# Four half tiles of the gated layer placed in the last attention round, the last output tiles on two banks, the lookup decode one chunk later

## The chip, the cores and the metric

The kernel runs on one core of a Trainium2 chip. The metric is the time of one execution on the device in microseconds, and the median of several executions is compared. The profile shows one further execution. Engines are named as in the profile: PE is TensorE (the matrix engine), DVE is VectorE, ACT is ScalarE, POOL is GpSimd, and SP issues most of the DMA transfers.

## The reference

Eight sequences of 256 tokens (2048 tokens in all, width 512) run through a tower of five stages, each with a residual sum and, from the second on, a layer norm of its input. What matters here are the last two:

```python
# stage 4: block attention, 16 heads of 128
q, k, v = hidden @ Wq, hidden @ Wk, hidden @ Wv      # per head
p = softmax(mask(q @ k.T * D ** -0.5))               # 256 tokens: the gate keeps every earlier block
h = h + (p @ v).reshape(B, S, H * D) @ Wo
# stage 5: gated feed-forward whose weights are looked up in a table of 16 floats
x = layernorm(h)
gate = x @ lut[gate_idx].T                           # 512 -> 1376
up   = x @ lut[up_idx].T                             # 512 -> 1376
h = h + (silu(gate) * up) @ lut[down_idx].T          # 1376 -> 512
```

Every product of the last two stages is made of f16 halves: both operands are split into a high and a low half, and three matmuls (high by high, high by low, low by high) stand for one in full precision.

## The kernel before, in words

**Tiles and chunks.** `h` holds all 2048 tokens as 16 tiles of 128. A chunk is 512 tokens, so there are four. The layer norm of a tile is a short chain over four engines: DVE takes statistics (L503 or L1247), aggregates (L509) and adds the epsilon (L511); POOL takes the power -0.5 (L516); DVE writes the normed rows (`ln_dve_x`, L525); PE transposes them in four matmuls (`ln_pe`, L536); ACT writes the high half (`ln_act`, L544) and DVE the low half (`ln_dve_lo`, L551) of `tokT`, which is what the next projections read.

**Block attention.** `mo_rounds` (L1142) is a loop in hardware over two pairs of head groups (`Fori` over p = 0, 1). One pair is 8 steps (s) of 4 rounds (j), written out. A round on PE (`mo_pe`, L1152) holds: the next round's query projection (L239, 12 matmuls), one value projection (L1101, 12), the next key projection (12) with the transposes of this round's probabilities inside it (L261, 6), probabilities by values (`mo_pv`, L1135 and L1138, 12 small ones), one output tile of the step before (`mo_out`, L1114, 12) and the next round's scores (L251 and L253, 12). DVE and ACT do softmax and the splits beside it. In the last two steps of the last pair each round also transposes a layer norm tile of the next stage (chunks 0 and 1), under an `If` that the first pair skips. In the last step of the last pair there are no value projections, and in its last round (s = 7, j = 3) no next round at all: PE waits for the probabilities, transposes them, waits for their split, does `mo_pv`, the output tile and one layer norm transpose.

**Between the stages.** Behind the rounds come, on PE, the four layer norm transposes of chunk 2 and the last four output tiles (`mo_out_tail`, L1119, line of its matmuls L1127), in banks 7, 6, 2 and 3 of PSUM. DVE adds each to `h` (`mo_dve_acc`, L1219), then takes the layer norm of chunk 3.

**Gated layer.** The 1376 hidden units are 11 tiles in three groups of 4, 4 and 3. A step t is one group for one chunk, 12 steps in all. `gl_pe_proj(t)` (L1271, matmuls L1289) makes for each hidden tile m a gate half and an up half, 12 matmuls each, in banks 0 and 1 for even tiles and 2 and 3 for odd ones; ACT takes the silu (L1313), DVE the product (L1327), ACT the high half (L1317), DVE the low half (L1329). `gl_pe_out(t)` (L1296, matmuls L571 in `out_tile`) makes four output tiles in banks 6, 7, 6, 7; the third waits until DVE has added the first to `h` (`accumulate`, L576), the fourth waits for the second. PE's order is proj(0), proj(1), out(0), proj(2), out(1) and so on. DVE's is the same idea one step shifted: the tiles of step t, then the four additions of step t-1. Chunk 3's layer norm transposes stand behind the hidden tiles of step 1.

**Lookup decode.** Weights of groups 0 and 1 were decoded long before; POOL splits them to halves (`gl_w`, L899 and L903; group 0 inside the second pair of attention, group 1 after the last layer norm). The 18 blocks of group 2 are decoded by DVE during the gated layer. `gdec_step(t, at)` (L2005) is called behind each hidden tile (at = 0 to 3) and each addition (at = 4 to 7) of step t, and writes out by hand which block b is masked (L859 to L864), spread (L873) and picked (L881) there; POOL splits each block (L890, L892) and counts `gfree`. PE waits for all 18 (`gfree`) ahead of proj(8). The indices come by one DMA (L1838), which SP issues once all attention outputs are there. SP's later transfers are one weight load (L1840) and the stores of the result (L1844, L1847).

The `If` that runs in the last pair only is this helper; ahead of the transposes a wait on the layer norm count stands under it:

```python
def last_pair(eng, p, pairs):
    return eng.If(p > pairs - 2)
```

## Time and profile before

| | |
|---|---|
| median of 3 executions | 2463.64 us (2461.04 to 2465.51) |
| profiled execution, its own time | 2462.3 us |
| its span | 2460.3 us |
| PE busy | 2323.6 us, 94% |
| DVE, ACT, POOL busy | 67%, 32%, 15% |
| chain that ended last | PE 80%, DVE 12%, ACT 4% |

Times in rows are microseconds from the start of the span. A row of a timeline gives the start, the length, engine, line, operation, tiles and shapes, the count of instructions merged in it, and in brackets the idle time ahead of it with what ended it. PE's instructions are pipelined: the next group starts a little before the modelled end of the one in front, so the pace is read from start to start.

### The profile page before, as it was taken

To read this page: it belongs to the slowest core of one execution; us is meant where nothing else is said; L and a number is where in the kernel's file an instruction comes from. 1 tells how busy PE (TensorE), PEld (TensorE's weight loads), DVE (VectorE), ACT (ScalarE), POOL (GpSimd) and SP (SyncE) were. 2 spreads that over 40 slices of the span, in tenths; PEclk is the share of its full clock that TensorE was granted. 3 is DMA by queue.
4 is the path that set the end of the run, shared out by engine and by line. 5 is a ranking of instruction groups with operands and counts; after the bars stand their busy time and mean duration, and the time that the engine had idled before them with its cause. 6 is when DMAs were issued, how large, how long until landed. Compare 5 with 4: busy or idle time off the path is not lost.

```text
span 2460.3 us, 32611 instructions
## 1 busy us (share of the span) xinstructions
PE 2323.6 (94%) x12610; PEld 1202.9 (49%) x12610; DVE 1654.4 (67%) x3165; ACT 788.6 (32%) x1683; POOL 376.2 (15%) x416
## 2 busy tenths in 40 slices
PE   5877799999999999889999999999999997999999
PEld 3666444444444444434455555555555554444444
DVE  6577599998999787676465555555555565778623
ACT  5576412122121113333343333333333332211111
POOL 2353100000000412630040004002100300411000
PEclk9898899999999999999999999999999998999999
DMA  4554623333332440200020001001100100100001
GB/s 161 171 172 171 227 92 114 125 121 114 122 120 86 163 165 33 78 31 19 27 69 1 1 1 69 1 2 35 35 1 1 52 1 1 56 1 1 1 1 69
DMA packets 50799, 166.71 MB, mean 68 GB/s; under 512 B 4048, under 2 KB 16976, under 8 KB 41680
## 3 DMA queue, kind: packets, MB, share of 16 engines
q1 hardware_dynamic: 50640, 164.56, 18.9%
q8 instruction: 103, 1.69, 0.3%
q14 instruction: 56, 0.46, 0.1%
HBM read 137.28 MB, written 27.26 MB: 67 GB/s over the span
## 4 chain that ended last, share of the span: by engine, by line
PE 80%; DVE 12%; ACT 4%; issue 2%; POOL 1%; DMA 1%; SPq 0%; DVEq 0%; ACTq 0%
PE ps L678 19%; PE ps L239 13%; PE ps L1289 7%; PE ps L690 7%; PE ps L1114 6%; PE ps L1101 6%; PE ps L571 4%; PE ps L929 3%; PE ps L946 3%; PE ps L1135 2%; PE ps L253 2%; PE ps L408 2%; PE ps L261 2%; PE ps L251 1%; PE ps L536 1%
## 5 line engine op out<-in xcount | busy, mean ns | idle before, releaser
L678 PE MATMUL ps<-planes 128*128 128x512 f16 x1224 | 270.0, 379 | 1.4 <-DVE work L735 1.4
L678 PE MATMUL ps<-planes,wa 128*128 128x512 f16 x1080 | 239.2, 380 | 5.2 <-DMA wa<-rw 5.2
L239 PE MATMUL ps<-planes,wa 128*128 128x512 f16 x840 | 201.5, 385 | 5.1 <-DVE planes L1576 5.1
L678 PEld LDWEIGHTS ps<-planes 128*128 128x128 f16 x1224 | 119.5, 98 | 143.4 <-DVE work L735 2.3
L239 PE MATMUL ps<-planes 128*128 128x512 f16 x768 | 180.9, 379 | 1.5 <-issue 1.5
L718 ACT ACTIVATE work<-work 128x512 f16<-128x512 f32 x64 | 40.3, 630 | 442.2 <-DVE work L751 442.2
L678 PEld LDWEIGHTS ps<-planes,wa 128*128 128x128 f16 x1080 | 106.0, 98 | 131.6 <-issue 7.5
L516 POOL TENSOR_TENSOR rstd<-rstd,half 128x4 f32<-128x4 f32 x16 | 17.1, 1071 | 871.1 <-DVE rstd L511 871.1
L294 ACT ACTIVATE ps<-ps,nmax 128x128 f32<-128x128 f32 x160 | 54.5, 341 | 295.4 <-DVE nmax L288 295.3
L833 DVE COPY_PREDICATED work<-work 128x1024 f32<-128x1024 int16 x144 | 120.4, 836 | 21.6 <-DVE work L833 0.8
L946 PE MATMUL ps<-wa,work 128*128 128x512 f16 x512 | 124.6, 387 | 9.0 <-DVE h L976 9.0
L815 DVE TENSOR_SCALAR work<-work,lutx,par 128x256 int32<-128x256 int32 x384 | 132.7, 421 | 0.0
L929 PE MATMUL ps<-planes,wa 128*128 128x512 f16 x512 | 126.0, 391 | 4.0 <-POOL wa L1059 4.0
L239 PEld LDWEIGHTS ps<-planes,wa 128*128 128x128 f16 x840 | 83.2, 99 | 93.2 <-issue 5.7
L1289 PE MATMUL ps<-planes 128*128 128x512 f16 x528 | 116.9, 379 | 2.6 <-DVE work L1327 2.6
L1289 PE MATMUL ps<-planes,wa 128*128 128x512 f16 x528 | 116.6, 379 | 0.0
L239 PEld LDWEIGHTS ps<-planes 128*128 128x128 f16 x768 | 75.1, 98 | 78.7 <-issue 1.7
L318 DVE TENSOR_TENSOR work<-ps,work 128x768 f16<-128x768 f32 x76 | 72.7, 956 | 47.4 <-ACT work L314 47.4
L1219 DVE TENSOR_TENSOR h<-ps,h 128x512 f32<-128x512 f32 x64 | 44.3, 692 | 83.5 <-PE ps L1114 76.9
L966 DVE TENSOR_TENSOR work<-work 128x512 f16<-128x512 f32 x64 | 49.1, 778 | 74.4 <-ACT work L962 74.4
L899 POOL TENSOR_SCALAR planes<-stg 128x512 f16<-128x512 f32 x44 | 30.9, 728 | 437.8 <-PE ps L1114 416.5
L301 DVE RECIPROCAL rinv<-rsum 128x4 f32<-128x4 f32 x80 | 14.2, 177 | 120.0 <-ACT ps L296 120.0
(193 smaller groups left out, 4442.3 us busy)
## 6 DMA issues: line engine op xcount, KB each, us to landing
planes<-rw SPq DMA_DIRECT2D x17, 2048.0 KB, 7.9
wa<-rw SPq DMA_DIRECT2D x15, 2048.0 KB, 7.3
stg<-in_rw_w SPq DMA_DIRECT2D x32, 512.0 KB, 3.8
stg<-in_ff_w SPq DMA_DIRECT2D x16, 1024.0 KB, 5.1
rw<-wa SPq DMA_DIRECT2D x16, 1024.0 KB, 7.0
stg<-in_mo_w SPq DMA_DIRECT2D x16, 1024.0 KB, 4.8
work<-in_glu_idx SPq DMA_DIRECT2D x48, 128.0 KB, 2.1
glu_dec<-work SPq DMA_DIRECT2D x48, 128.0 KB, 1.7
```

The costliest lines, as they stand in the source:

```text
L239: mm = te.matmul(ps[:, bank, :], w(i, kt), x(j, kt), start=(kt == 0 and n == 0), stop=(kt == KT - 1 and n == 2))
L318: ve.tensor_tensor(pT[1].rearrange("p (b k) -> p b k", b=2), pT_view, pT[0].rearrange("p (b k) -> p b k", b=2), ALU.subtract).then_inc(pT_ ...
L571: mm = te.matmul(ps[:, bank, :], x, y, start=(m == 0), stop=(m == len(pairs) - 1))
L678: mm = te.matmul(ps[:, what, :], rw_w(q, what, i, kt, m), mix[what][j][:, kt, at:at + CH], start=(kt == 0 and z == 0), stop=(kt == KT - 1 ...
L690: mm = te.matmul(ps[:, 4 + j, :], oT[t % 4][x][:, j * P:j * P + P], rw_wo(q, y, m), start=(n == 0 and z == 0), stop=(n == HEADS - 1 and z ...
L815: return ve.tensor_scalar(dec_v[:, j, :].bitcast(I32), dec_idx, lutx[:, j:j + 1], lut[:, 2 * j:2 * j + 1], ALU.bitwise_and, ALU.bitwise_xor)
L833: ins = ve.copy_predicated(pairs[:, :, 0, :], mask, pairs[:, :, 1, :])
L929: mm = te.matmul(ps[:, t % 3, :], slot[:, at:at + P], tokT[x][:, kt, c * CH:c * CH + CH], start=(kt == 0 and x == 0), stop=(kt == KT - 1 a ...
L946: mm = te.matmul(ps[:, 4 + j, :], gT[t % FF_BUF][x][:, j * P:j * P + P], slot[:, PW + m * D:PW + m * D + D], start=(k == 0 and x == 0), st ...
L1101: mm = te.matmul(ps[:, bank, :], tokT[x][:, kt, tt * P:tt * P + P], halves(slot, 2)[y][:, kt * CH:kt * CH + CH], start=(kt == 0 and z == 0 ...
L1114: mm = te.matmul(ps[:, FB, :], x, y, start=(z == 0), stop=(z == len(pairs) - 1))
L1289: mm = te.matmul(ps[:, bank, :], glu_halves(g, piece)[i][:, at:at + P], tokT[j][:, kt, c * CH:c * CH + CH], start=(kt == 0 and z == 0), st ...
```

## The change

It has three parts. Four half tiles of proj(0) (gate and up of hidden tiles 0 and 1) leave `gl_pe_proj` and are placed one by one: both halves of tile 0 ahead of the probability transposes of the last round, the gate half of tile 1 between these and `mo_pv`, the up half of tile 1 behind the rounds; their silus, products and splits are placed between the layer norm pieces of chunk 2. The last four output tiles use banks 7, 6, 7, 6, so the third and fourth wait for the additions of the first and second, each tile is placed one place earlier relative to the transposes, and the wait for all four additions, which stood ahead of hidden tile 1, stands ahead of out(0). `gdec_step` starts one step later: block 0 at the additions of step 1, and blocks 16 and 17 at the hidden tiles of step 7.

```diff
@@ -1114,7 +1114,7 @@
                 mm = te.matmul(ps[:, FB, :], x, y, start=(z == 0), stop=(z == len(pairs) - 1))
             mm.then_inc(mw_ps, 1)
 
-        TAIL_BANK = [FB, OB, 2, 3]
+        TAIL_BANK = [FB, OB, FB, OB]
 
         def mo_out_tail(pe, tt, slot):
 
@@ -1122,6 +1122,8 @@
             if tt == 0:
                 pe.wait_ge(mo_lo, n)
                 pe.wait_ge(mw_acc, n + 4)
+            if tt >= 2:
+                pe.wait_ge(mw_acc, n + 4 + tt - 1)
             pairs = [(oH[1][j][x][:, tt * P:tt * P + P], halves(slot, 3)[y][:, j * D:j * D + D]) for j in range(4) for x, y in PASSES]
             for z, (x, y) in enumerate(pairs):
                 mm = te.matmul(ps[:, TAIL_BANK[tt], :], x, y, start=(z == 0), stop=(z == len(pairs) - 1))
@@ -1166,7 +1168,12 @@
             if rcond is None:
                 mo_q(pe, *nround, 1, transposes)
             else:
+                with last_pair(pe, p, MO_PAIRS):
+                    gl_pe_part(pe, 0, 0, 0)
+                    gl_pe_part(pe, 0, 0, 1)
                 transposes()
+                with last_pair(pe, p, MO_PAIRS):
+                    gl_pe_part(pe, 0, 1, 0)
                 with Maybe(pe, rcond):
                     mo_q(pe, *nround, 1)
             mo_pv(pe, p, s, j)
@@ -1268,34 +1275,36 @@
         def gl_rows(g, m):
             return G_LAST if g == 2 and m == 2 else P
 
+        def gl_pe_part(pe, t, m, piece):
+            g, c = GL_T[t]
+            n = gl_base(t) + m
+            if m == 0 and piece == 0 and c == 0:
+                if g < 2:
+                    pe.wait_ge(w_ready, WR_GL + 3 * g + 3)
+                else:
+                    pe.wait_ge(gfree, GDEC_BLOCKS)
+            if n >= 2 and piece == 0:
+                pe.wait_ge(prod_sb, n - 1)
+            for kt in range(KT):
+                for z, (i, j) in enumerate(PASSES):
+                    at = kt * G_TILES[g] * P + m * P
+                    mm = te.matmul(ps[:, 2 * (n % 2) + piece, :], glu_halves(g, piece)[i][:, at:at + P],
+                                   tokT[j][:, kt, c * CH:c * CH + CH], start=(kt == 0 and z == 0),
+                                   stop=(kt == KT - 1 and z == 2))
+            mm.then_inc((ga_ps, up_ps)[piece], 1)
+
         def gl_pe_proj(pe, t):
-            g, c = GL_T[t]
-            if c == 0 and g < 2:
-                pe.wait_ge(w_ready, WR_GL + 3 * g + 3)
-            elif c == 0:
-                pe.wait_ge(gfree, GDEC_BLOCKS)
-            for m in range(G_TILES[g]):
-                n = gl_base(t) + m
-                if n >= 2:
-                    pe.wait_ge(prod_sb, n - 1)
-                elif n == 1:
-                    pe.wait_ge(mw_acc, 8 + 64)
-                W = G_TILES[g] * P
-                for piece, done in ((0, ga_ps), (1, up_ps)):
-                    bank = 2 * (n % 2) + piece
-                    for kt in range(KT):
-                        for z, (i, j) in enumerate(PASSES):
-                            at = kt * W + m * P
-                            mm = te.matmul(ps[:, bank, :], glu_halves(g, piece)[i][:, at:at + P],
-                                           tokT[j][:, kt, c * CH:c * CH + CH], start=(kt == 0 and z == 0),
-                                           stop=(kt == KT - 1 and z == 2))
-                    mm.then_inc(done, 1)
+            for m in range(2 if t == 0 else 0, G_TILES[GL_T[t][0]]):
+                gl_pe_part(pe, t, m, 0)
+                gl_pe_part(pe, t, m, 1)
                 if t == 1:
                     ln_pe(pe, 3, 3, m)
 
         def gl_pe_out(pe, t):
             g, c = GL_T[t]
             pe.wait_ge(gl_lo, gl_base(t + 1))
+            if t == 0:
+                pe.wait_ge(mw_acc, 8 + 64)
             for j in range(TPC):
                 pairs = []
                 for m in range(G_TILES[g]):
@@ -1303,30 +1312,42 @@
                     pairs += [(hT[t % 2][m][x][0:r, j * P:j * P + P], glu_halves(g, 2)[y][0:r, m * D:m * D + D]) for x, y in PASSES]
                 out_tile(pe, O_GL + 4 * t + j, 6 + j % 2, pairs)
 
+        def gl_act_silu(act, t, m):
+            n = gl_base(t) + m
+            act.wait_ge(ga_ps, n + 1)
+            if n >= 2:
+                act.wait_ge(gl_lo, n - 1)
+            se.activation(sg_buf[n % 2], ps[:, 2 * (n % 2), :], ACT.Silu).then_inc(silu_sb, 1)
+
+        def gl_act_hi(act, t, m):
+            n = gl_base(t) + m
+            act.wait_ge(prod_sb, n + 1)
+            if m == 0 and t >= 2:
+                act.wait_ge(wo_ps, O_GL + 4 * t)
+            se.activation(hT[t % 2][m][0], sg_buf[n % 2], ACT.Copy).then_inc(gl_hi, 1)
+
         def gl_act(act, t):
-            g, c = GL_T[t]
-            for m in range(G_TILES[g]):
-                n = gl_base(t) + m
-                act.wait_ge(ga_ps, n + 1)
-                if n >= 2:
-                    act.wait_ge(gl_lo, n - 1)
-                se.activation(sg_buf[n % 2], ps[:, 2 * (n % 2), :], ACT.Silu).then_inc(silu_sb, 1)
-                act.wait_ge(prod_sb, n + 1)
-                if m == 0 and t >= 2:
-                    act.wait_ge(wo_ps, O_GL + 4 * t)
-                se.activation(hT[t % 2][m][0], sg_buf[n % 2], ACT.Copy).then_inc(gl_hi, 1)
+            for m in range(2 if t == 0 else 0, G_TILES[GL_T[t][0]]):
+                gl_act_silu(act, t, m)
+                gl_act_hi(act, t, m)
                 if t == 1:
                     ln_act(act, 3, 3, m)
 
+        def gl_dve_prod(dve, t, m):
+            n = gl_base(t) + m
+            dve.wait_ge(silu_sb, n + 1)
+            dve.wait_ge(up_ps, n + 1)
+            ve.tensor_tensor(sg_buf[n % 2], sg_buf[n % 2], ps[:, 2 * (n % 2) + 1, :], ALU.mult).then_inc(prod_sb, 1)
+
+        def gl_dve_lo(dve, t, m):
+            n = gl_base(t) + m
+            dve.wait_ge(gl_hi, n + 1)
+            ve.tensor_tensor(hT[t % 2][m][1], sg_buf[n % 2], hT[t % 2][m][0], ALU.subtract).then_inc(gl_lo, 1)
+
         def gl_dve(dve, t, between):
-            g, c = GL_T[t]
-            for m in range(G_TILES[g]):
-                n = gl_base(t) + m
-                dve.wait_ge(silu_sb, n + 1)
-                dve.wait_ge(up_ps, n + 1)
-                ve.tensor_tensor(sg_buf[n % 2], sg_buf[n % 2], ps[:, 2 * (n % 2) + 1, :], ALU.mult).then_inc(prod_sb, 1)
-                dve.wait_ge(gl_hi, n + 1)
-                ve.tensor_tensor(hT[t % 2][m][1], sg_buf[n % 2], hT[t % 2][m][0], ALU.subtract).then_inc(gl_lo, 1)
+            for m in range(2 if t == 0 else 0, G_TILES[GL_T[t][0]]):
+                gl_dve_prod(dve, t, m)
+                gl_dve_lo(dve, t, m)
                 if t == 1:
                     ln_dve_lo(dve, 3, 3, m)
                 between(t, m)
@@ -1932,7 +1953,13 @@
             ln_chunk(act, ln_act, 2, NC - 1)
             act_exp(act, MU)
             mo_rounds(act, lambda *x: mo_act(act, *x))
-            ln_chunk(act, ln_act, 3, 2)
+            gl_act_silu(act, 0, 0)
+            gl_act_silu(act, 0, 1)
+            ln_act(act, 3, 2, 0), ln_act(act, 3, 2, 1)
+            gl_act_hi(act, 0, 0)
+            ln_act(act, 3, 2, 2)
+            gl_act_hi(act, 0, 1)
+            ln_act(act, 3, 2, 3)
             for t in range(len(GL_T)):
                 gl_act(act, t)
 
@@ -1992,20 +2019,24 @@
 
             mo_rounds(dve, lambda *x: mo_dve(dve, *x, chain))
             ln_chunk(dve, ln_dve_x, 3, 2)
+            mo_dve_acc(dve, MO_PAIRS, 0, 0, TAIL_BANK[0])
+            gl_dve_prod(dve, 0, 0)
             ln_dve_lo(dve, 3, 2, 0), ln_dve_lo(dve, 3, 2, 1)
-            mo_dve_acc(dve, MO_PAIRS, 0, 0, TAIL_BANK[0])
+            mo_dve_acc(dve, MO_PAIRS, 0, 1, TAIL_BANK[1])
+            gl_dve_prod(dve, 0, 1)
+            gl_dve_lo(dve, 0, 0)
             ln_dve_lo(dve, 3, 2, 2)
-            mo_dve_acc(dve, MO_PAIRS, 0, 1, TAIL_BANK[1])
+            mo_dve_acc(dve, MO_PAIRS, 0, 2, TAIL_BANK[2])
+            gl_dve_lo(dve, 0, 1)
             ln_dve_lo(dve, 3, 2, 3)
-            mo_dve_acc(dve, MO_PAIRS, 0, 2, TAIL_BANK[2])
             mo_dve_acc(dve, MO_PAIRS, 0, 3, TAIL_BANK[3])
             dve.wait_ge(mw_acc, 8 + 64)
             ln_dve_chunk(dve, 3, 3, chain)
             ln_chunk(dve, ln_dve_x, 3, 3)
             def gdec_step(t, at):
 
-                b = 3 * t - 2 + (at // 2 if at < 4 else 2) if t > 0 else 0
-                if b < GDEC_BLOCKS and (t > 0 or at >= 4):
+                b = 3 * t - 5 + (at // 2 if at < 4 else 2)
+                if 0 <= b < GDEC_BLOCKS:
                     if at in (0, 2, 4):
                         gdec_dve_mask(dve, b)
                     if at in (0, 2, 5):
@@ -2041,12 +2072,13 @@
                     pe.wait_ge(mv_lo, j + 1)
                 ln_pe(pe, 2, NC - 1, j)
             mo_rounds(pe, lambda *x: mo_pe(pe, *x))
+            gl_pe_part(pe, 0, 1, 1)
+            mo_out_tail(pe, 0, weight_slot("moba", 1))
             ln_pe(pe, 3, 2, 0), ln_pe(pe, 3, 2, 1)
-            mo_out_tail(pe, 0, weight_slot("moba", 1))
+            mo_out_tail(pe, 1, weight_slot("moba", 1))
             ln_pe(pe, 3, 2, 2)
-            mo_out_tail(pe, 1, weight_slot("moba", 1))
+            mo_out_tail(pe, 2, weight_slot("moba", 1))
             ln_pe(pe, 3, 2, 3)
-            mo_out_tail(pe, 2, weight_slot("moba", 1))
             mo_out_tail(pe, 3, weight_slot("moba", 1))
             gl_pe_proj(pe, 0)
             for t in range(len(GL_T)):
```

## Rows read from the trace of the kernel before

**Rows 1.** The page: busy time and share of the engines, and TensorE's granted clock.

```profile
PE 2323.6 (94%) x12610; PEld 1202.9 (49%) x12610; DVE 1654.4 (67%) x3165; ACT 788.6 (32%) x1683; POOL 376.2 (15%) x416
...
PEclk9898899999999999999999999999999998999999
```

**Rows 2.** TensorE's timeline, last attention round: start, length, work [idle before].

```profile
2058.26 0.87 PE L261 MATMUL ps<-ident,work 128*128 128x128 f32 x6 [1.94 <-DVE work L307]
...
2061.18 0.50 PE L1135 MATMUL ps<-work,planes 128*128 128x256 f16 x3
...
2062.18 2.75 PE L1114 MATMUL ps<-wa,planes 128*128 128x512 f16 x12
...
2065.87 0.49 PE L253 MATMUL ps<-work 128*128 128x256 f16 x3
2071.53 1.52 PE L261 MATMUL ps<-ident,work 128*128 128x128 f32 x6 [5.17 <-DVE work L307]
2074.95 0.82 PE L1135 MATMUL ps<-work,planes 128*128 128x256 f16 x3 [1.90 <-DVE work L318]
```

**Rows 3.** The same, from the end of the rounds into the gated layer.

```profile
2080.22 0.60 PE L536 MATMUL ps<-ident,work 128*128 128x128 f32 x4
2085.12 1.89 PE L536 MATMUL ps<-ident,work 128*128 128x128 f32 x8 [4.30 <-DVE work L525]
2086.80 3.68 PE L1127 MATMUL ps<-wa,planes 128*128 128x512 f16 x12
2090.32 0.60 PE L536 MATMUL ps<-ident,work 128*128 128x128 f32 x4
2090.75 2.75 PE L1127 MATMUL ps<-wa,planes 128*128 128x512 f16 x12
...
2098.96 26.06 PE L1289 MATMUL ps<-planes 128*128 128x512 f16 x120
```

**Rows 4.** Two stretches of 10 us: busy by engine, then granted clock, DMA.

```profile
2070.00:2080.00 10.00, 6.57 (x29) 3.93 (x30) 4.00 (x7) 1.62 (x4) 0.00 (x0) 0.66 0.00 0
2150.00:2160.00 10.00, 4.70 (x13) 1.54 (x12) 9.20 (x22) 1.11 (x2) 1.14 (x2) 0.68 0.00 0
```

**Rows 5.** VectorE's timeline around the end of the rounds.

```profile
2070.80 0.68 DVE L307 TENSOR_TENSOR work<-ps,rinv 128x512 f32<-128x512 f32 x1
...
2084.52 1.92 DVE L525 TENSOR_SCALAR work<-h,mv,rstd 128x512 f32<-128x512 f32 x4 [1.12 <-POOL rstd L516]
...
2099.16 0.69 DVE L1219 TENSOR_TENSOR h<-ps,h 128x512 f32<-128x512 f32 x1 [1.90 <-PE ps L1127]
...
2104.10 3.09 DVE L525 TENSOR_SCALAR work<-h,mv,rstd 128x512 f32<-128x512 f32 x4 [1.12 <-POOL rstd L516]
```

**Rows 6.** TensorE's waits from 2100 us to the end: total, times, longest.

```profile
PE ps L571 <- DVE h L576: 8.1, 6, 5.3
PE ps L1289 <- DVE work L1327: 2.6, 2, 2.1
```

**Rows 7.** TensorE's timeline, outputs of chunk 0 and the projection behind them.

```profile
2155.70 7.63 PE L571 MATMUL ps<-planes,work 128*128 128x512 f16 x24 [5.30 <-DVE h L576]
2163.17 20.88 PE L1289 MATMUL ps<-planes 128*128 128x512 f16 x96
```

**Rows 8.** VectorE's timeline, one decode instruction beside GpSimd's splits and without them.

```profile
2123.80 1.19 DVE L862 TENSOR_SCALAR planes<-planes 128x256 int16<-128x256 int16 x1
...
2135.51 0.22 DVE L862 TENSOR_SCALAR planes<-planes 128x256 int16<-128x256 int16 x1
```

**Rows 9.** GpSimd's timeline: last split of group 0's weights, last lookup block.

```profile
1930.02 4.50 POOL L903 TENSOR_TENSOR planes<-stg,planes 128x512 f16<-128x512 f32 x4
...
2317.01 0.67 POOL L892 TENSOR_TENSOR stg<-planes,stg 128x256 f16<-128x256 f32 x1
```

**Rows 10.** ScalarE's timeline: its table load ahead of the first silu.

```profile
2094.60 1.28 ACT L1313 ACT_TABLE_LOAD   x1
```

**Rows 11.** TensorE's timeline where the loop over pairs goes back.

```profile
1651.94 2.75 PE L239 MATMUL ps<-planes 128*128 128x512 f16 x12 [1.47 <-issue]
```

## The prediction

> **What bounds the kernel.** I read the page first. PE is busy 94% of the span and its granted clock is 9 or 8 tenths almost everywhere [rows 1], so what can be gained lies in PE's waits, and in stretches at the low clock behind them. I then went along PE's timeline over the place that the diff touches. Up to the last round PE runs with short gaps: in the round before, transposes, probabilities by values and an output tile follow on each other at the full pace [rows 2]. In the last round there is nothing to put between them. PE waits 5.17 us for DVE's probabilities and 1.90 us for their split [rows 2], and behind the rounds 4.30 us for the layer norm rows of chunk 2 [rows 3]. The granted clock of that stretch is 0.66 [rows 4], between the levels of 1.2 and 2.4 GHz, and what follows each wait is slow: 6 transposes take 1.52 us, not 0.87 [rows 2], and an output tile 3.68 us [rows 3]. Last, PE's waits behind 2100 us come to two lines only: the output tiles wait 8.1 us in 6 places for DVE's additions, once 5.3 us, and the projections 2.6 us for its products [rows 6]. The 5.3 us end at 2155.70, and there again the clock is down (0.68 over ten microseconds, [rows 4]; 24 matmuls take 7.63 us, [rows 7]). PE alone sets the end from the last round on, so a microsecond off its waits is one off the time, as long as no other wait grows.
>
> **Part 1: the half tiles and the tail.** The pace of the gated layer is 26.06 us for 120 matmuls [rows 3], 0.217 each: 2.61 us for 12, 5.21 for 24. An output tile has the same 12 shapes, so 2.61 too. A set of 4 transposes takes 0.43 (2090.32 to 2090.75, [rows 3]), the 12 of `mo_pv` 1.00 (2061.18 to 2062.18) and the 6 transposes some 0.70 (0.87 less the 0.17 by which such a row overlaps the next, [rows 2, 3]). No matmul is added or removed. From the end of the last scores, 2066.36 (2065.87 and 0.49, [rows 2]), to the end of proj(0), 2119.8 (2098.96 and 96 x 0.217, [rows 3]), PE now takes 53.4 us. Its work at full pace is 8 half tiles 20.9, 4 tail tiles 10.4, the round's output tile 2.6, five sets of layer norm transposes 2.2, `mo_pv` 1.0, transposes 0.7: 37.8 us. If nothing waits and the clock holds, 15.6 us go: 11.4 us are the three waits, 4.2 us the low clock.
>
> Does anything wait? I lay the new order out. Two half tiles fill 2066.36 to 2071.5; the probabilities are ready when the last normalization ends, 2070.80 and 0.68 [rows 5]. So that wait is filled nearly exactly (0.1 us may stay). The half tile behind the transposes runs to some 2074.9. DVE needs the transposes' end, ACT's copy and its own split, 1.9 us of wait in all at the row's start of 2074.95; with transposes that start alike and run faster the split is there at 2074.2, so `mo_pv` starts 0.7 us later than it could, which costs nothing, since PE works. `mo_pv`, output tile and transposes then end at 2079.0 where they end now at 2080.82 (2080.22 and 0.60, [rows 3]). From that end to the first layer norm row of chunk 2 the chain over DVE and POOL takes 3.7 us to its start (2084.52, [rows 5]) and a quarter of 1.92 us more: ready at 2083.3. PE has the up half of tile 1 and the first tail tile in front, 5.2 us, to 2084.1. Slack 0.8 us: thin, and the first thing that could be late. Its price is one for one. The third and fourth tail tiles now wait for additions. DVE's order puts the first behind the four rows (2084.7), and two transposes and a tile stand between on PE until 2087.9; slack over 2 us. The layer norm transposes of tile 2 need the low half of tile 0, behind that addition and one product, near 2086.7, against 2087.6: 0.9 us. ACT has the table load, 1.28 us [rows 10], and two silus ahead of its next layer norm copy: from 2079.7 to 2082.2, and the copy is due at 2084.7. The last tail tile ends at 2093.7, not 2099.16 as now (start of the last addition, [rows 5]). Chunk 3's layer norm on DVE then takes as now to 2107.2 from 2099.16 (2104.10 and 3.09, [rows 5]), 8.0 us, so to 2101.7, and hidden tile 2's product stands behind it, near 2102.4. PE needs it at the first tile of proj(1), 2104.1. Slack 1.7 us. Weights of group 0 lie ready since 1934.5 (1930.02 and 4.50, [rows 9]), 130 us ahead. Bank 0 and 1 are free, since the last round projects no query or key. Part 1: -15.5 us.
>
> **Part 2: the decode.** In the kernel before, block 0 starts on DVE right behind the last product of step 0, while POOL is still splitting weights; one decode instruction takes 1.19 us there and 0.22 later without them [rows 8]. The block stands ahead of step 1's products, and blocks 1 and 2 between them, and the 2.6 us and the 5.3 us of waits are theirs [rows 6]. Moved a step on, step 1 has no decode until its additions. DVE's share of a hidden tile there is product, low half and layer norm half, under 3 us against PE's 5.6, so the first addition of out(0) is bound by its own tile and is done 1.8 us before PE's third tile wants it. Both waits go: 7.9 us. With them goes the low clock behind the second, 7.47 (2155.70 to 2163.17) less 5.21: 2.3 us [rows 7]. Idle figures count from a modelled end that lies 0.17 us past the pace, three times 0.5 us more. Part 2: -10.7 us. In return the decode reaches into step 7. Steps 2 to 6 now pay (8.1 - 5.3) / 5 = 0.56 us each, since the third output tile waits for an addition that stands behind a pick [rows 6]; steps 2 to 7 will, one more: +0.7 us with its 0.17. The wait for `gfree` ahead of proj(8) has its cover: the last block's split ends at 2317.68 in step 6 now [rows 9], about when PE takes up its last two output tiles, 5.2 us before the next projection. One step on it is the same. SP and its DMAs keep their order; the index load starts some 5 us earlier and is due 30 us later.
>
> **Part 3: the branches.** PE gets two new `If`s, which pair 0 skips (24 and 12 matmuls). No row has a jump of that length by itself. The nearest rows: the jump back of the loop costs 1.47 us of issue [rows 11], as upper bound each; at the `If` around 4 layer norm transposes, which pair 0 skips eight times, the same timeline shows no idle time: lower bound zero, and a gain is excluded, as instructions are only added. I take 0.3 us for both, since PE's queue is full there; 2.9 us goes into the range. The Trainium skill (Runtime: NRT & Kernel Launch, Instruction fetch mechanics) says that a taken branch beyond the window already fetched must first fetch its target. By it the sum would be the 1.47 for each jump that leaves the window: -22.6 us in place of -25.2 if both do.
>
> **The sum**: -15.5 - 10.7 + 0.7 + 0.3 = -25.2 us against the profiled execution's own 2462.3, so 2437.1. The median shown is 1.3 us above that execution: 2463.64 - 25.2 = 2438.4.
>
> **The rivals.**
> - A: a thin slack closes (layer norm rows of chunk 2, or the low half behind the first product) and each such wait gives back 1 to 3 us, with the clock down behind it as now. For it: 0.8 and 0.9 us are small against the chain of four engines. Against: all lengths are from rows. 5 us back: 2443.4.
> - B: the stalls of step 1 don't go but move, since DVE now meets step 1 with POOL's splits still running, or to out(1). For it: DVE is the releaser of every wait there. Against: ten microseconds of decode leave it. Half of part 2 back, 5.4, to all, 10.7: 2443.8 to 2449.1.
> - C: the skipped branches cost their upper bound, twice 1.47: 2441.0.
> - D: the change doesn't fill the round, because a half tile waits for something that I take as ready, and DVE's and ACT's new order only passes the waits on. Part 2 alone stays: 2463.64 - 10.7 + 0.7 = 2453.6. Against: the weights are ready 130 us ahead, and the tokens' norm is two steps back.
> - E, on the other side: the granted clock. The stretch from 2066 us on becomes nearly gapless. If PE were then granted 1.2 GHz for a long time, each such microsecond would cost half of one; beyond 50 us of it the whole gain is spent, beyond 60 us the kernel is slower than 2468.6. Against: of the 40 slices the dense ones already show 9 [rows 1], and low clock shows behind waits, not behind work [rows 4].
>
> **How the numbers follow.** My forecast has 0.62, A 0.12, B 0.10, C 0.08, D 0.04, E 0.03, and 0.01 lies elsewhere. The forecast's own range is the 2.3 us that the runs scatter on either side, and 1 us of fractions: 2435 to 2442. The 8 in 10 take in C, A and the near end of B: 2434.5 to 2446. A measurement of this kernel can tell about 0.2%, 5 us, from no change: all cases but E lie below that, D by 10 us. Faster 0.95, same 0.02, slower 0.03.
>
> **What would show it.** Right: PE without a wait over 0.3 us from the last scores to the end of out(0), the granted clock at 1.00 in ten-microsecond stretches there, proj(0) ending near 2104, proj(2) starting near 2137 in place of 2163.17 [rows 7]; six waits of 0.56 us on additions in steps 2 to 7; proj(8) without a wait. Wrong: a wait for L525 ahead of the layer norm transposes (A), one for L576 or L1327 over 1 us in step 1 (B), issue time on PE near the end of pair 0's last round (C), idle time ahead of the first half tile (D), a slice with a low clock and no idle time (E).

## The result, and the profile after

| | before | changed |
|---|---|---|
| median (range) | 2462.57 us (2461.04 to 2465.51, 4 runs) | 2438.0 us (2435.26 to 2441.05, 4 runs) |
| profiled execution | 2462.3 us | 2440.1 us (one of the four) |
| last scores of attention to start of proj(2) | 96.81 us | 70.37 us |
| start of proj(2) to PE's last matmul | 293.99 us | 294.73 us |

The ratio is 0.9896 (95% interval 0.9882 to 0.991): 24.6 us less. The prediction was 2438.4, range 2434.5 to 2446. The median before has one run more in it than the 2463.64 that the prediction started from. The last two lines of the table are read from PE's timelines: the first is from the end of the last row of L253 to the first projection behind out(0) [rows 2, 7]. They are the yardstick of everything below. The three stages ahead of attention scatter by several microseconds from one execution to the next (the first value projection of attention starts at 1218.1 us before, at 1221.7 here, and between 1215.1 and 1223.3 in the profiles of the experiments), in code that no kernel here touches; the two stretches repeat to 0.1 us in most kernels, and the exceptions have a cause, told below.

PE's timeline of the changed kernel, from the last scores to the end of out(0) and proj(2), answers to [rows 2, 3, 7]; the lines are start, length, work:

```profile
2069.37 0.49 PE L253 MATMUL ps<-work 128*128 128x256 f16 x3
2069.70 5.34 PE L1291 MATMUL ps<-planes 128*128 128x512 f16 x24
2075.03 0.88 PE L261 MATMUL ps<-ident,work 128*128 128x128 f32 x6
2075.74 2.75 PE L1291 MATMUL ps<-planes 128*128 128x512 f16 x12
...
2079.32 2.75 PE L1114 MATMUL ps<-wa,planes 128*128 128x512 f16 x12
...
2084.93 2.75 PE L1129 MATMUL ps<-wa,planes 128*128 128x512 f16 x12
2087.53 1.04 PE L536 MATMUL ps<-ident,work 128*128 128x128 f32 x8
...
2097.04 15.70 PE L1291 MATMUL ps<-planes 128*128 128x512 f16 x72
2129.87 10.52 PE L571 MATMUL ps<-planes,work 128*128 128x512 f16 x48
2140.23 20.88 PE L1291 MATMUL ps<-planes 128*128 128x512 f16 x96
...
2166.84 5.35 PE L571 MATMUL ps<-planes,work 128*128 128x512 f16 x24 [0.55 <-DVE h L576]
```


No line from 2069.37 to 2140.23 has idle time in brackets. The transposes of the probabilities take 0.88 us, the first tail tile 2.75, not 3.68 as in [rows 3]. out(0) is one row of 48 matmuls; before it was cut by 5.30 us. The wait for an addition, 0.55 us, stands in out(1) and the steps behind it.

The same place by stretches of ten microseconds (columns as in [rows 4], the granted clock third from the end):

```profile
2070.00:2080.00 10.00, 10.00 (x58) 5.20 (x57) 5.22 (x11) 3.01 (x10) 0.00 (x0) 1.00 0.00 0
2080.00:2090.00 10.00, 10.00 (x54) 5.34 (x53) 7.02 (x17) 4.80 (x8) 1.01 (x1) 1.00 0.01 2
```


And all of PE's waits over 0.2 us from 2060 us on, to set beside [rows 6] (the second line belongs to the round before the last, which no kernel here changes):

```profile
PE ps L571 <- DVE h L576: 3.4, 6, 0.6
PE ps L261 <- DVE work L307: 1.9, 1, 1.9
```


The thin places, first on DVE's timeline of the changed kernel (compare [rows 5]):

```profile
2086.21 1.92 DVE L525 TENSOR_SCALAR work<-h,mv,rstd 128x512 f32<-128x512 f32 x4 [1.12 <-POOL rstd L516]
...
2089.23 1.28 DVE L551 TENSOR_TENSOR planes<-ps,planes 128x512 f16<-128x512 f32 x2
...
2105.19 0.67 DVE L1340 TENSOR_TENSOR work<-work,ps 128x512 f32<-128x512 f32 x1
2106.55 1.39 DVE L1345 TENSOR_TENSOR work<-work 128x512 f16<-128x512 f32 x1 [0.69 <-ACT work L1327]
```

And on ACT's timeline, the table load and the first layer norm copy of chunk 2 (compare [rows 10]):

```profile
2083.16 1.28 ACT L1320 ACT_TABLE_LOAD   x1
...
2088.16 1.08 ACT L544 ACTIVATE planes<-ps 128x512 f16<-128x512 f32 x2 [2.62 <-PE ps L536]
```


The first layer norm row of chunk 2 is ready at 2086.7 (2086.21 and a quarter of 1.92), and PE takes it at 2087.53. Tile 0's low half is written at 2089.9, and PE's next transposes are due at 2090.99. Tile 0's silu waits for nothing but its table load, and the layer norm copy behind it is on time at 2088.16. Hidden tile 2's product ends at 2105.86; PE's first tile of proj(1) is due some 48 x 0.217 = 10.4 us behind 2097.04, at 2107.45.

### The profile page after: what moved, and what is told of

The parts are those of the page before. It is cut to its first block, busy times and chain, and to the rows that moved or that the text cites. A ratio compares the mean times of both kernels' runs of the same rounds, so it can differ in the third digit from the quotient of the medians.

```text
span 2438.1 us, 32615 instructions
## 1 busy us (share of the span) xinstructions
PE 2317.2 (95%) x12610; PEld 1200.4 (49%) x12610; DVE 1650.1 (68%) x3165; ACT 787.9 (32%) x1683; POOL 374.0 (15%) x416
## 4 chain that ended last, share of the span: by engine, by line
PE 81%; DVE 10%; ACT 4%; POOL 2%; issue 2%; DMA 1%; SPq 0%; DVEq 0%; ACTq 0%
PE ps L678 20%; PE ps L239 13%; PE ps L1291 8%; PE ps L690 7%; PE ps L1114 6%; PE ps L1101 6%; PE ps L571 3%; PE ps L929 3%; PE ps L946 3%; PE ps L1137 2%; PE ps L253 2%; PE ps L261 2%; PE ps L408 2%; PE ps L536 1%; PE ps L251 1%
```

## The experiments

Times are medians beside runs of the kernel before on the same chip; "the stretch" is last scores to proj(2) in the profile, "the rest" from there to PE's last matmul. Experiments 1, 4, 5, 8 and 9 start from the changed kernel, 2, 3, 6 and 7 from the one before. Kernels 4 and 6 were profiled twice; the second profiled executions took 2440.39 and 2461.9 us.

| | median, us | ratio (95%) | stretch | rest |
|---|---|---|---|---|
| before | 2461.4 to 2463.4 | 1 | 96.81 | 293.99 |
| changed, run again | 2437.04 | 0.9895 (0.9877 to 0.9913) | 70.36 | 294.67 |
| 1 half tiles and tail only | 2451.67 | 0.9958 (0.9945 to 0.9971) | 85.98 | 294.01 |
| 2 decode shift only | 2449.7 | 0.9951 (0.9938 to 0.9964) | 85.66 | 294.72 |
| 3 tail order only | 2460.1 | 0.9988 (0.9979 to 0.9996) | 92.55 | 294.00 |
| 4 hidden tile 0 only | 2443.01 | 0.9919 (0.9907 to 0.9931) | 74.39, 76.06 | 294.68 |
| 5 pick behind the addition | 2433.12 | 0.9877 (0.9859 to 0.9896) | 70.38 | 290.30 |
| 6 first wait filled | 2463.68 | 1.0006 (0.9997 to 1.0015) | 96.19, 96.37 | 293.93 |
| 7 all waits filled | 2457.95 | 0.998 (0.9971 to 0.9989) | 92.80 | 293.91 |
| 8 block 0 in step 0 | 2445.15 | 0.993 (0.9914 to 0.9946) | 79.25 | 293.95 |
| 9 the same, splits behind it | 2435.13 | 0.9886 (0.9871 to 0.9901) | 70.37 | 293.93 |

The changed kernel's second runs were expected so:

> The changed kernel itself, run beside the next three as their yardstick. Both theories: as measured, 24 to 25 us under before.

They came out so (2437.04, 24.4 us under 2461.39), with the stretch equal to 0.01 us.

### 1 and 2: each part alone

```diff
 # 1, against the changed kernel
-                b = 3 * t - 5 + (at // 2 if at < 4 else 2)
-                if 0 <= b < GDEC_BLOCKS:
+                b = 3 * t - 2 + (at // 2 if at < 4 else 2) if t > 0 else 0
+                if b < GDEC_BLOCKS and (t > 0 or at >= 4):
 # 2, against the kernel before: the same two pairs of lines, the other way round
```

> The changed kernel with the decode schedule of before (block 0 at the additions of step 0). My theory: part 1 is worth 15.5 us by itself, but block 0 now meets POOL's splits for its whole length and DVE is 0.6 us further behind PE, so the waits of step 1 stay and grow by about 1.5 us: near 2448.5 us, 14 us under before, with a wait of L1291 for DVE of 2 to 4 us and one of L571 of some 5 us. Rival (the parts simply add): 15.5 us under before, and the waits of step 1 as they were. Rival (most of the gain is the decode's): less than 8 us under before.

> The kernel of before with the decode one step later and nothing else. My theory: the 2.6 us and 5.3 us of waits in step 1 and the low clock behind them go, a sixth wait of 0.56 us comes: 10 us under before, near 2452.6 us. Rival B of the prediction (the stall moves to out(1) or the next step): 0 to 5 us under before.

Alone, the half tiles bring 10.3 us (2461.97 less 2451.67; 10.8 of the stretch) and the decode 12.3 (11.2 of the stretch, less 0.7 of the rest). The two savings add to 22.0, while both changes together take 26.4 off the stretch: 4.5 us exist only if both are made. Kernel 1 is where they went. PE's timeline of it, from the second transposes of chunk 3 on:

```profile
2113.63 0.60 PE L536 MATMUL ps<-ident,work 128*128 128x128 f32 x4
2121.40 6.85 PE L1291 MATMUL ps<-planes 128*128 128x512 f16 x24 [7.17 <-DVE work L1340]
...
2143.90 7.54 PE L571 MATMUL ps<-planes,work 128*128 128x512 f16 x24 [4.42 <-DVE h L576]
```


Its first wait of step 1 is 7.17 us, where the kernel before has 2.13 (of the 2.6 us in [rows 6]), and the low clock comes with it (a row of 24 matmuls takes 6.85 us, at full pace 5.34). I had expected 2 to 4 us. DVE's and POOL's timelines show why, first in the kernel before:

```profile
2122.00 0.70 DVE L859 CAST planes<-planes 128x256 int16<-128x256 int32 x1
...
2122.64 4.54 POOL L903 TENSOR_TENSOR wa<-stg,wa 128x512 f16<-128x512 f32 x4
...
2127.31 2.67 DVE L873 TENSOR_SCALAR planes<-planes,lutx,par 128x256 int32<-128x256 int32 x8
```

and in kernel 1:

```profile
2105.97 0.70 DVE L859 CAST planes<-planes 128x256 int16<-128x256 int32 x1
...
2115.63 6.13 POOL L903 TENSOR_TENSOR wa<-stg,wa 128x512 f16<-128x512 f32 x4
...
2115.73 5.04 DVE L881 COPY_PREDICATED planes<-planes 128x1024 f32<-128x1024 int16 x3
```

The parts don't add: PE reaches step 1 some 15 us sooner against the scores. Block 0 started 5.2 us before the splits ended in the kernel before and took 10.6 us (2122.00 to 2132.6). In kernel 1 it lies wholly beside them and takes 14.8 (2105.97 to 2120.8). The median is 3.2 us over the 2448.5 that I expected. Kernel 2 came out as expected in kind, with no wait in step 1, and a little better in size.

### 3 and 4: pieces of the first part

```diff
 # 3, against the kernel before: banks 7, 6, 7, 6, and each tail tile one place earlier
-            ln_pe(pe, 3, 2, 0), ln_pe(pe, 3, 2, 1)
             mo_out_tail(pe, 0, weight_slot("moba", 1))
+            ln_pe(pe, 3, 2, 0), ln_pe(pe, 3, 2, 1)
...
 # 4, against the changed kernel: tile 1 back in proj(0)
-                with last_pair(pe, p, MO_PAIRS):
-                    gl_pe_part(pe, 0, 1, 0)
...
-            gl_pe_part(pe, 0, 1, 1)
...
-            for m in range(2 if t == 0 else 0, G_TILES[GL_T[t][0]]):
+            for m in range(1 if t == 0 else 0, G_TILES[GL_T[t][0]]):
```

> The kernel of before with the last four output tiles each one place earlier and on banks 7, 6, 7, 6, no half tile moved, decode as before. My theory: the first tail tile (2.6 us) covers that much of the 4.3 us wait for the layer norm rows, and with it some low clock: 3 to 4.5 us under before, near 2459 us, and no wait ahead of the third and fourth tile. Rival: these two now wait for additions and give it back: within 1 us of before.

> The changed kernel with hidden tile 0 alone moved early (the two half tiles ahead of the transposes); both halves of tile 1 are back in their place. My theory: the wait ahead of the value products is open again (1.9 us less what the faster transposes save, so 1.2 to 1.9) and the wait for the layer norm rows is 4.3 less the tail tile's 2.6, so 1.7; the clock stays up: 3 to 3.6 us over the changed kernel, near 2441.3 us. Rival: the granted clock falls again behind these waits and adds 2 to 4 us: near 2444.5 us.

Kernel 3 has a stretch 4.3 us shorter, as my theory said; its median shows 1.9, with runs scattered over 8.6 us and the stages ahead of attention ending 4.9 us later in its profile than in that of before (1223.0 against 1218.1). The first tail tile does not start at once, but the wait for rows of chunk 2 is down from 4.30 to 1.11 us, plus 0.44 us until the round's last addition. The third and fourth tile wait for nothing. Kernel 4 is 4.0 us over the changed one by the stretch, 5 by the medians of different sets; the three waits open again, in PE's timeline of its first profile:

```profile
2072.94 0.50 PE L1137 MATMUL ps<-work,planes 128*128 128x256 f16 x3 [1.89 <-DVE work L318]
...
2077.57 2.75 PE L1129 MATMUL ps<-wa,planes 128*128 128x512 f16 x12 [0.44 <-DVE h L1224]
2081.43 1.11 PE L536 MATMUL ps<-ident,work 128*128 128x128 f32 x8 [1.11 <-DVE work L525]
```


1.89, 0.44 and 1.11 make 3.4, and three pipeline ends of 0.17 the rest. In this profile the clock stayed up. A second profile of the same kernel had the same three waits and a stretch of 76.06:

> The kernel with hidden tile 0 alone moved early, one more look, for the same question: fixed by the program: full pace behind the 1.9 us wait again (74.4 us from the last scores to proj(2)). Not fixed: the low clock shows there this time, and 2 to 4 us more.

PE's timeline of that second profile:

```profile
2072.47 0.50 PE L1137 MATMUL ps<-work,planes 128*128 128x256 f16 x3 [1.90 <-DVE work L318]
...
2072.98 0.73 PE L1137 MATMUL ps<-work,planes 128*128 128x256 f16 x3
...
2073.83 4.07 PE L1114 MATMUL ps<-wa,planes 128*128 128x512 f16 x12
```


The value products begin at full pace (0.50) and go on at the low one (0.73), and the output tile takes 4.07 us, not 2.75. So with short waits left in place, whether the clock falls differs between executions of one program.

### 6 and 7: the clock by itself

```diff
 # against the kernel before; 6 has the first block with filler(pe, 0), filler(pe, 1) of 12 matmuls each
+        def filler(bank, n):
+            for x in range(n):
+                te.matmul(ps[:, bank, :], glu_halves(0, 0)[0][:, x * P:x * P + P], tokT[0][:, 0, 0:CH], start=(x == 0), stop=(x == n - 1))
...
+                with last_pair(pe, p, MO_PAIRS):
+                    pe.wait_ge(w_ready, WR_GL + 3)
+                    filler(0, 12)
+                    filler(1, 12)
                 transposes()
+                with last_pair(pe, p, MO_PAIRS):
+                    filler(0, 8)
...
             mo_rounds(pe, lambda *x: mo_pe(pe, *x))
+            filler(0, 9)
+            filler(1, 9)
```

> The kernel of before with 24 matmuls more (the shapes of two half tiles, their result in banks 0 and 1 never read) in the 5.17 us wait of the last round; all real work stays where it was, the decode too. It prices the clock by itself. My theory: the low clock of that stretch was caused by the idle time, so with the wait filled the transposes, the value products and the output tile behind it run at full pace (2.4 us less), and the second wait too may end sooner: 2.4 to 4.1 us under before, though 5.2 us of work are added. Rival: the clock has nothing to do with it, or the added work only delays: 0 to 1 us over before.

> The kernel with the first wait filled, one more look. If the fall of the clock behind the 1.9 us wait is fixed by the program, the value products run at the low clock again (a row of 3 takes 0.7 us or more). If it hangs on something that differs from execution to execution, they may run at full pace (0.50), as in the kernel with tile 0 alone moved, whose PE work is the same up to there.

> The kernel of before with added matmuls of no use in all three waits (24, 8 and 18 of the 512-column shape), the decode as before. The run with the first wait alone filled gave back only 0.7 us from the last scores to the start of proj(0), since the clock fell behind the second wait instead. My theory now: the low clock belongs to the row of waits, not to one, so with all three covered the whole stretch is at full pace: 4 us less from the last scores to the start of proj(0) (28.6 us in place of 32.6), granted clock 1.00 there. Rival: the clock falls in this place whatever fills it, or the added work makes its own delay: 32 us or more.

With the first wait covered (kernel 6) the way from the last scores to proj(0) is 31.95 and 31.96 us in the two profiles, not 32.60 (2066.36 to 2098.96, [rows 2, 3]): 0.65 us saved, not the 2.4 I expected, and the median shows no gain. The transposes run at full pace, but the clock falls behind the second wait, at once in one profile and within the value products in the other. PE's timeline of the first:

```profile
2064.00 5.34 PE L1155 MATMUL ps<-planes 128*128 128x512 f16 x24
2069.34 0.87 PE L261 MATMUL ps<-ident,work 128*128 128x128 f32 x6
2072.11 0.74 PE L1135 MATMUL ps<-work,planes 128*128 128x256 f16 x3 [1.89 <-DVE work L318]
...
2073.92 3.61 PE L1114 MATMUL ps<-wa,planes 128*128 128x512 f16 x12
```


With all three covered (kernel 7) the waits that are left are 0.17 and 0.41 us, and everything up to proj(0) runs at full pace. PE's timeline:

```profile
2072.32 1.89 PE L1154 MATMUL ps<-planes 128*128 128x512 f16 x8
2074.38 0.50 PE L1135 MATMUL ps<-work,planes 128*128 128x256 f16 x3 [0.17 <-DVE work L318]
...
2078.41 4.05 PE L1154 MATMUL ps<-planes 128*128 128x512 f16 x18
2082.87 1.11 PE L536 MATMUL ps<-ident,work 128*128 128x128 f32 x8 [0.41 <-DVE work L525]
2083.82 2.75 PE L1127 MATMUL ps<-wa,planes 128*128 128x512 f16 x12
```


From the last scores to proj(0) it is 28.6 us, and the stretch is 92.80, both 4.0 us less than before (the median is 5.4 less, 2457.95 against 2463.40), with 50 useless matmuls more and not one piece of work moved. This is the clock's share of part 1, which the prediction had put at 4.2 us, now measured without the rest. Covering the first wait alone gave 0.65 us of it. Kernel 4 kept the clock in one of its two profiles with waits of 1.89, 0.44 and 1.11 us left, so filling every wait is not always needed; no kernel here covers the second or the third wait alone.

### 8 and 9: what block 0 costs

```diff
 # 8, against the changed kernel
-                b = 3 * t - 5 + (at // 2 if at < 4 else 2)
-                if 0 <= b < GDEC_BLOCKS:
+                b = 3 * t - 4 + (at // 2 if at < 4 else 2) if t > 0 else 0
+                if at >= 4 if t < 2 else b < GDEC_BLOCKS:
 # 9, besides: POOL's program
+            gdec_pool_split(pool, 0)
             gl_w(1)
-            for b in range(GDEC_BLOCKS):
+            for b in range(1, GDEC_BLOCKS):
```

> The changed kernel with only block 0 of the decode back at the additions of step 0, beside POOL's splits; block 1 at the additions of step 1, the rest three per step, block 17 alone in step 7. It tells block 0's place from that of blocks 1 and 2 among step 1's hidden tiles. My theory: the first of the two waits of step 1 comes back (2.5 to 3.5 us, with POOL beside it), the 5.3 us one does not, and one wait of 0.56 us goes: 2 to 3 us over the changed kernel. Rival: block 0 is what delays all of step 1: the 5 us wait and the low clock come back too: 7 to 10 us over the changed kernel.

> The kernel with block 0 in step 0 (8.9 us slower than the changed one from the last scores to proj(2)), and POOL's splits of group 1 moved behind block 0's own split, so that they no longer run beside block 0. Theory of contention: block 0 then takes some 6.5 us on DVE where it took 14.9 beside the splits, the 7.2 us wait of proj(1) goes to under 1 us, and the kernel is within 1.5 us of the changed one (70.4 us from the last scores to proj(2)). Rival of place: any block between the products of step 0 and step 1 delays PE: at least 4 us over the changed kernel.

Block 0 alone in step 0 costs 8.9 us of the stretch, far over my 2 to 3. The size is the rival's, but not its mechanism: out(0) is whole, and the cost is one wait of 7.19 us and 1.5 us of low clock behind it. DVE's timeline of kernel 8 shows why, with POOL's last split beside it:

```profile
2107.51 0.70 DVE L859 CAST planes<-planes 128x256 int16<-128x256 int32 x1
...
2110.16 7.08 DVE L873 TENSOR_SCALAR planes<-planes,lutx,par 128x256 int32<-128x256 int32 x8
2117.18 6.14 POOL L903 TENSOR_TENSOR wa<-stg,wa 128x512 f16<-128x512 f32 x4
2117.28 5.05 DVE L881 COPY_PREDICATED planes<-planes 128x1024 f32<-128x1024 int16 x3
2122.23 0.68 DVE L1340 TENSOR_TENSOR work<-work,ps 128x512 f32<-128x512 f32 x1
...
2141.70 2.67 DVE L873 TENSOR_SCALAR planes<-planes,lutx,par 128x256 int32<-128x256 int32 x8
```

From 2107.51 block 0 lasts until 2122.3, 14.8 us, with the eight instructions of the spread in 7.08 us and the picks in 5.05. POOL splits without a pause from 2099.09 to 2123.3. The spread of block 1, one step later and with POOL idle, takes 2.67. And DVE's timeline of kernel 9, where POOL's splits stand behind the block (the last line is their first):

```profile
2104.17 0.29 DVE L859 CAST planes<-planes 128x256 int16<-128x256 int32 x1
...
2105.23 2.67 DVE L873 TENSOR_SCALAR planes<-planes,lutx,par 128x256 int32<-128x256 int32 x8
2107.94 2.55 DVE L881 COPY_PREDICATED planes<-planes 128x1024 f32<-128x1024 int16 x3
2110.39 0.68 DVE L1340 TENSOR_TENSOR work<-work,ps 128x512 f32<-128x512 f32 x1
...
2111.70 2.80 POOL L899 TENSOR_SCALAR wa<-stg 128x512 f16<-128x512 f32 x4
```


Here the block takes 6.3 us, spread 2.67, picks 2.55. The product that PE waits for is written at 2111.1 in kernel 9, in time, and the stretch is 70.37, the same as the changed kernel's, with the block still in step 0. (Block 1 then meets the last split, its spread takes 5.42 us, but it stands between additions and nobody waits.) So block 0's cost was neither its place nor its work but the company. That is block 0 alone: kernels 1 and 8 differ only in the places of the other blocks, and the stretch by 6.7 us (85.98 against 79.25). Blocks 1 and 2 between the hidden tiles of step 1 cost that, by the 4.42 us wait of out(0) and 2.2 us of low clock behind it. Whether they would still cost it with POOL's splits out of the way was not tried.

### 5: what the changed kernel leaves

```diff
 # against the changed kernel: hidden tile 3 runs no decode; behind the additions stand
+                    if j == 0:
+                        gdec_step(t, 3)
+                    elif j == 1:
+                        gdec_step(t, 4), gdec_step(t, 5)
+                    elif j == 2:
+                        gdec_step(t, 6)
```

> The changed kernel with DVE's order turned at each step's end: the pick of the second block behind the first addition, mask and spread of the third behind the second addition. My theory: the first addition no longer stands behind a pick, so the six waits of 0.56 us of the third output tile go, each with its 0.15 of pipeline: 4.3 us under the changed kernel, near 2433.7 us. Rival: the second addition, now behind the pick, is late for the fourth tile instead: within 1 us of the changed kernel, with waits of L571 at other tiles.

4.4 us off the rest, and 3.9 us off the changed kernel's median of the same set: 2433.12, ratio to before 0.9877. DVE adds as soon as the output tile is there, and the pick fits in front of the second addition. DVE's timeline at out(2):

```profile
2196.43 0.69 DVE L576 TENSOR_TENSOR h<-ps,h 128x512 f32<-128x512 f32 x1
2197.03 2.55 DVE L881 COPY_PREDICATED planes<-planes 128x1024 f32<-128x1024 int16 x3
2199.47 0.69 DVE L576 TENSOR_TENSOR h<-ps,h 128x512 f32<-128x512 f32 x1
```


Its PE timeline has no wait over 0.2 us between the last scores and the end. This is the lowest median of the study; kernel 9, at 2435.13 beside another set, lies within the scatter of it, and the two were not put together.

## Why the prediction was right

**Part 1.** The prediction had 53.4 us from the last scores to the end of proj(0) become 37.8, and set -15.5 us. After: 2069.86 to 2107.45, 37.6 us; -15.8. The order that was laid out by hand holds piece by piece. Foreseen slacks were 0.8 us for the first layer norm row, 0.9 for tile 0's low half and 1.7 for hidden tile 2's product; they came out as 0.8, 1.1 and 1.6. The split into 11.4 us of waits and 4.2 of clock was an argument then, and kernel 7 measured the clock's share at 4.0.

**Part 2.** Set at -10.7 us; the stretch of 26.4 less part 1's 15.8 leaves 10.6. By the prediction proj(2) starts 70.6 us behind the last scores (2137 less 2066.36), and it came at 70.37. The sixth wait came as set: 6 waits of 3.4 us in all, and 0.7 us more of the rest. The wait for the last block stays covered: proj(8) starts without one. What the prediction had only half right is the cause. It named POOL's contention from one instruction (1.19 against 0.22, [rows 8]) but counted block 0 as a place in DVE's order. Kernels 8 and 9 show that block 0 in that same place costs 8.9 us beside the splits and nothing without them. In the kernel before less of it showed: only the five instructions of block 0's mask met the end of the splits and took 5.3 us (2122.00 to 2127.3), against 1.0 in kernel 9 (2104.17 to 2105.2); spread and picks ran at their full pace.

**Part 3.** The skipped branches were set at 0.3 us with 2.9 as the bound. The attention rounds up to the last scores take 848.18 us from the first value projection, 848.23 before, with two jumps more, and the jump back still costs 1.47 us of issue. In the last round of pair 0, where the two branches are skipped, PE's timeline has no idle time. The same way takes 847.4 to 848.7 us in the other profiles, 848.55 and 848.73 in kernels 2 and 3, which have no branch; so 0.3 us can't be told from nothing here, and 2.9 can. Rival C falls. The Trainium skill (Runtime: NRT & Kernel Launch, Instruction fetch mechanics) has a taken branch wait for a fetch if its target is not in the window. No run here shows where the two targets lay; by the unchanged 848.2 us no such wait reached PE's work.

**The rivals A, B, D and E** did not come. D would have shown as idle time ahead of the first half tile, and there is none at 2069.70. A was a matter of 0.8 us. B came true in kernel 1, which has the half tiles and not the decode shift: there the stall grows to 7.17 us. E falls with ten-microsecond stretches at a granted clock of 1.00 throughout.

**The sum** was -25.2 us and the measured median -24.6, the second set -24.4. The two stretches show 25.7 (26.4 less 0.7), against 25.5 set for them without the branches. That the median lies within 0.4 us of 2438.4 is luck in part: the four runs are 2435.3, 2435.9, 2440.1 and 2441.1, and the profiled one is only 22.2 us under that of before, as its attention starts 3.6 us later (1221.7 against 1218.1). My expectations for the experiments did worse than the prediction: kernel 1's wait, kernel 6's gain and kernel 8's cost were each off by 2 to 6 us. They were about the parts one at a time, where a wait that is left pulls the clock down or meets POOL. The prediction was about both at once, where no wait is left.

**Open:** why the stages ahead of attention scatter by up to 8 us. Their granted clock between 1000 and 1100 us lies between 0.91 and 0.96 in these profiles, lower where attention starts late (0.91 at 1223.3, 0.96 at 1216.4). Which of the two brings the other is not shown; nothing here was tried on it.

## What to carry to other kernels

Work that does not depend on a chain belongs into the chain's waits, one piece sized for each wait, and it pays twice when it covers all of them, since the clock then held in every profile here; covering the longest alone gave 0.65 us of 4. Before moving a step of DVE for its place, look at what GpSimd does beside it: moving GpSimd's work behind the step gave the same stretch here (70.37 us), and 0.8 us less of the rest, where one wait fewer is left. Two changes that feed the same engine must be judged together: alone these two took 22.0 us off the stretch, together 26.4.

## What the runs showed of the hardware

Beside GpSimd's splits (kernel 8, against the same instructions without them in kernels 8 and 9) DVE was slower by factors that depend on the instruction: the spread (one input in SBUF) 7.08 against 2.67 us, the predicated copies 5.05 against 2.55, the low half (two inputs in SBUF) 1.39 against 0.69, while the product with one input in PSUM kept its 0.67. GpSimd was slowed too: four of its instructions at L903 took 6.14 us beside the predicated copies, and 4.5 to 5.0 elsewhere. The Trainium skill (GPSIMD Engine Reference, Specifications) has the SBUF interfaces shared with VectorE, with contention for VectorE instructions that have two SBUF inputs or run in a 2-port mode; the low half agrees with it by its 1.39 us and the product by its 0.67. No run here shows in which mode the spread ran.

The granted clock fell behind a wait of 1.89 or 1.90 us in three of four profiles of two kernels (4 and 6) that have the same shapes of PE's work up to there, 24 matmuls and 6 transposes without idle time in front, and did not in the fourth. The last three rounds before the last one, which have the same PE work in all kernels here, have a wait of 1.93 or 1.94 us each, ahead of their transposes. In 8 of these 42 waits of the 14 profiles the transposes behind took 1.11 to 1.50 us, in the others 0.87 to 0.90 (2058.26 in [rows 2] is one). PE's timeline of kernel 1 has one of the eight:

```profile
2055.79 1.19 PE L261 MATMUL ps<-ident,work 128*128 128x128 f32 x6 [1.93 <-DVE work L307]
```

So the fall is not fixed by the program, nor by the length of the wait alone. In kernel 4 it is worth 1.7 us (76.06 against 74.39). What decides it is open.
